# Target rows as three bfloat16 parts, one wait per gather pair, and one word of block numbers per chunk, in a graph attention and expert kernel

## The reference

```python
xl = (x @ W_l).reshape(n, H, C)          # n = 6250, H = 4, C = 64
xr = (x @ W_r).reshape(n, H, C)
feat = xl[src] + xr[dst]                 # 106250 edges, sorted by dst
feat = jnp.where(feat >= 0, feat, NEG_SLOPE * feat)
logits = jnp.einsum('ehc,hc->eh', feat, att)
seg_max = jax.ops.segment_max(logits, dst, num_segments=n)
ex = jnp.exp(logits - seg_max[dst])
seg_sum = jax.ops.segment_sum(ex, dst, num_segments=n)
alpha = ex / (seg_sum[dst] + 1e-16)
out = jax.ops.segment_sum(alpha[:, :, None] * xl[src], dst, num_segments=n)
```

## Time and profile before

| | us |
|---|---|
| median of three runs | 2654.8 (2643.6 to 2661.4) |
| the profiled execution, whole | 2630.2 |
| its span, first to last instruction | 2628.4 |
| mean granted TensorE clock | 0.903 |

### The profile page before, as it was taken

How to read it: one execution, slowest core, us unless ns; L and a number is a source line. 1 busy time by engine, 2 the same in 40 slices (tenths; PEclk the granted TensorE clock), 3 DMA queues, 4 the chain that set the end, 5 groups by cost and what they waited for, 6 DMA issues and landing times. The chain is left out here.

```text
span 2628.4 us, 46465 instructions
## 1 busy us (share of the span) xinstructions
PE 2168.0 (82%) x9585; PEld 1785.7 (68%) x9586; DVE 1553.9 (59%) x3448; ACT 1211.0 (46%) x3043; POOL 1351.4 (51%) x1265
## 2 busy tenths in 40 slices
PE   3967898988898899989998889853957719999993
PEld 2755777777677777777777767732846718888883
DVE  5745777777777777777777777887455420111110
ACT  2433556556565666656565655543541102222220
POOL 3356565666566666656665665446003762444442
PEclk9988999999999999999999999975965559999997
DMA  7555555555555555555555555434043345666664
GB/s 216 179 179 148 137 148 137 151 144 146 139 149 148 141 142 152 147 143 137 149 143 142 140 148 138 105 109 145 21 133 110 88 120 153 144 144 144 143 143 123
DMA packets 280941, 365.73 MB, mean 139 GB/s; under 512 B 52329, under 2 KB 233218, under 8 KB 280762
## 3 DMA queue, kind: packets, MB, share of 16 engines
q1 hardware_dynamic: 191070, 194.14, 25.5%
q0 software_dynamic: 73984, 154.20, 25.2%
q10 hardware_dynamic: 15836, 16.81, 2.0%
HBM read 306.42 MB, written 64.88 MB: 141 GB/s over the span
## 5 line engine op out<-in xcount | busy, mean ns | idle before, releaser
L773 POOL DMA_INDIRECT ring<-xl_rows,a_idx x928 | 927.2, 999 | 598.2 <-issue 239.0
L1078 PE MATMUL a_f_ps<-a_xr_w,a_hot_n 128*128 128x268 f32 x1856 | 595.4, 403 | 37.2 <-issue 13.1
L1091 PE MATMUL a_o_ps<-ring,a_hot_e 128*128 128x264 f32 x1856 | 508.7, 398 | 95.9 <-DVE acc L976 83.8
L1080 PE MATMUL a_f_ps<-ring,ident 128*128 128x264 f32 x1856 | 581.1, 396 | 0.0
L946 DVE SCALAR_TENSOR_TENSOR a_pos<-a_f_ps,att_ext 128x528 f32<-128x528 f32 x464 | 325.0, 700 | 374.2 <-PE a_f_ps L1080 238.4
L1091 PEld LDWEIGHTS a_o_ps<-ring,a_hot_e 128*128 128x128 f32 x1856 | 343.3, 193 | 185.4 <-issue 119.5
L1078 PEld LDWEIGHTS a_f_ps<-a_xr_w,a_hot_n 128*128 128x128 f32 x1856 | 355.9, 196 | 104.4 <-issue 42.9
L1080 PEld LDWEIGHTS a_f_ps<-ring,ident 128*128 128x128 f32 x1856 | 363.9, 196 | 72.6
L854 ACT COPY a_lg<-a_f_ps 128x8 f32<-128x8 f32 x464 | 79.2, 171 | 549.8 <-DVE a_pos L946 421.5
L956 DVE TENSOR_REDUCE a_lg<-a_pos 128x8 f32<-128x528 f32 x464 | 322.2, 694 | 1.4 <-issue 0.4
L964 DVE TENSOR_TENSOR ring<-ring (+1 forms) x464 | 316.8, 683 | 0.0
(11 more groups left out here) (306 smaller groups left out, 2198.1 us busy)
## 6 DMA issues: line engine op xcount, KB each, us to landing
a_xr_w<-xr_rows SPq DMA_DIRECT2D x464, 134.0 KB
a_rel_bc<-rel_rows SPq DMA_DIRECT2D x232, 128.0 KB
x_w<-in_L_ffn_W_dram SPq DMA_DIRECT2D x56, 512.0 KB
ring<-xl_rows,a_idx POOLq DMA_INDIRECT x928
ring<-disp_rows SPq DMA_DIRECT2D x56, 257.0 KB
xr_rows<-xr_sb SPq DMA_DIRECT2D x50, 134.0 KB, 1.9
xl_rows<-xl_sb SPq DMA_DIRECT2D x50, 132.0 KB, 1.8
j_xl<-xl_rows SPq DMA_DIRECT2D x25, 264.0 KB, 2.8
```

What stands on the lines that cost most here:

```text
L773: nc.gpsimd.indirect_dma_start(xl_e[:, p * T + 2 * h + u, :], None, k.xl_rows, bass.IndirectOffsetOnAxis(ap=idx[:, p, 2 * h + u:2 * h + u ...
L1078: nc.tensor.matmul(f_ps[:, g, u, 0:XRW], hot_n[:, j % 2, 2 * g + u, :], xr_w[:, h % XR, :], start=True, stop=False)
L1080: last = nc.tensor.matmul(f_ps[:, g, u, 0:XW], k.ident[:, :], xl_e[:, p * T + 2 * h + u, :], start=False, stop=True)
L1091: last = nc.tensor.matmul(o_ps[:, hh % 2, 0:XW], hot_e[:, j % 2, 2 * g + u, :], xl_e[:, pp * T + 2 * hh + u, :], start=(u == 0), stop=(u = ...
```

## The change

It has four parts.

1. `project_nodes` splits the 268 columns of each `xr` row in three bfloat16 parts: high = bf16(xr) on ACT (L627 in the new file), mid = bf16(xr - high) on DVE (L584), rest = xr - high on POOL (L541), low = bf16(rest - mid) on POOL (L546). `xr_rows` in DRAM then has 3 x 268 bfloat16 columns, and the store waits for the low part. The rings of `xl_sb` and `xr_sb` grow from four to eight.
2. `attend` multiplies a `hot_n` that is now bfloat16 with the three parts, adding up in PSUM; the identity product and the sums stay f32. The old L1078 is L1141, the old L1080 is L1143.
3. `gather` on POOL waits for `sum_done` alone, and for `idx_ready` in the first unit of a chunk.
4. `prepare_edges` packs the 16 block numbers of a chunk into a word (a block number and 15 bits), stores `word_rows`, and SP in `attend` reads one word per chunk and gets the numbers by register arithmetic. Some semaphores of `prepare_edges` are joined.

```diff
 def prepare_edges
@@ sync
                 sp.dma_start(k.block_rows[0].rearrange("(g u) -> g u", g=SG), blk_t[:, :]).then_inc(stored, 16)
+                sp.wait_ge(words_then_gates, 1)
+                sp.dma_start(k.word_rows[0].rearrange("(g c) -> g c", g=SG), word_i[:, :]).then_inc(stored, 16)
                 sp.wait_ge(ends_stored, 64)
@@ vector
+                link(nc.vector.memset(rise_bit[:, 1:2], float(WORD_BASE)))
+                for n in (1, 2, 4, 8):
+                    at = min(n, NU - 1 - n)
+                    link(nc.vector.tensor_scalar(rise_bit[:, 1 + n:1 + n + at], rise_bit[:, 1:1 + at], float(2 ** n), None, ALU.mult))
...
                 scales(nc, k, dve, link, 0, LN_HALF)
+                link(nc.vector.tensor_copy(blk_f[:, :, :], blk_t[:, :].rearrange("g (c h) -> g c h", h=NU)))
+                link(nc.vector.tensor_tensor(rise[:, :, 1:NU], blk_f[:, :, 1:NU], blk_f[:, :, 0:NU - 1], ALU.subtract))
+                link(nc.vector.tensor_tensor(rise[:, :, 1:NU], rise[:, :, 1:NU],
+                                             rise_bit[:, None, 1:NU].to_broadcast([SG, P // 2 // NU, NU - 1]), ALU.mult))
+                link(nc.vector.tensor_copy(rise[:, :, 0], blk_f[:, :, 0]))
+                link(nc.vector.tensor_reduce(blk_f[:, :, 0], rise[:, :, :], AX.X, ALU.add))
+                nc.vector.tensor_copy(word_i[:, :], blk_f[:, :, 0]).then_inc(words_then_gates, 1)
                 dve.wait_ge(picked[1], 16 * SG)
 def project_nodes
@@ sync
-                    sp.wait_ge(xr_full, t + 1)
+                    sp.wait_ge(low_ready, t + 1)
...
-                    sp.dma_start(k.xr_rows[bass.ds(row, P), :], xr_sb[:, s, :]).then_inc(stored[s], 16)
+                    sp.dma_start(k.xr_rows[bass.ds(row, P), :], parts[:, s].rearrange("p a w -> p (a w)")).then_inc(stored[s], 16)
@@ gpsimd
+                def rest_of(t, s):
+                    pool.wait_ge(high_ready, t + 1)
+                    wait_past(pool, low_ready, t - 1)
+                    nc.gpsimd.tensor_tensor(rest[:, s % 2, :], xr_sb[:, s, :], parts[:, s, 0, :], ALU.subtract).then_inc(rest_ready, 1)
+
+                def low_part(t, s):
+                    pool.wait_ge(mid_ready, t + 1)
+                    pool.wait_ge(rest_ready, t + 1)
+                    nc.gpsimd.tensor_tensor(parts[:, s, 2, :], rest[:, s % 2, :], parts[:, s, 1, :], ALU.subtract).then_inc(low_ready, 1)
@@ vector, at the end of self_logits(t)
+                    if not isinstance(t, int) or t >= 1:
+                        mid_part(t - 1, (s - 1) % ROWS)
+
+                def mid_part(t, s):
+                    dve.wait_ge(high_ready, t + 1)
+                    nc.vector.tensor_tensor(parts[:, s, 1, :], xr_sb[:, s, :], parts[:, s, 0, :], ALU.subtract).then_inc(mid_ready, 1)
@@ scalar, at the end of take_x(t)
+                    if not isinstance(t, int) or t >= 1:
+                        high_part(t - 1, (s - 1) % ROWS)
+
+                def high_part(t, s):
+                    act.wait_ge(xr_full, t + 1)
+                    nc.scalar.copy(parts[:, s, 0, :], xr_sb[:, s, :]).then_inc(high_ready, 1)
 def attend
@@ gpsimd, gather
-                    wait_past(pool, sum_done, c * NU + (h - RING + 1))
-                    wait_past(pool, f_done, c * NU + (h - LANDS + 1))
-                    pool.wait_ge(idx_ready, c + 1)
+
+                    if isinstance(c, int) and c * NU + h < RING:
+                        wait_past(pool, f_done, c * NU + (h - LANDS + 1))
+                    else:
+                        pool.wait_ge(sum_done, c * NU + (h - RING + 1))
+                    if h == 0:
+                        pool.wait_ge(idx_ready, c + 1)
@@ sync, loads
+                    word = nc.values_load_multi_w_load_instructions(k.row_words[:, bass.ds(c, 1)], engines=[mybir.EngineType.SP],
+                                                                    min_val=0, max_val=WORD_HALF - 1)[1][0]
+                    blocks = blocks_of(word)
                     for j in range(QUADS):
+                        row_of = [nc.sync.compute_val(blocks[2 * j + g]) for g in range(2)]
...
-                        blocks = load_blocks(nc, k, mybir.EngineType.SP, c * NU + 2 * j, 2)
@@ tensor, logits_of
                     for u in range(2):
-                        nc.tensor.matmul(f_ps[:, g, u, 0:XRW], hot_n[:, j % 2, 2 * g + u, :], xr_w[:, h % XR, :],
-                                         start=True, stop=False)
+                        for a in range(PARTS):
+                            nc.tensor.matmul(f_ps[:, g, u, 0:XRW], hot_n[:, j % 2, 2 * g + u, :], xr_w[:, h % XR, a, :],
+                                             start=(a == 0), stop=False)
```

More of the change, by code:

```diff
@@ L469, in project_nodes @@
         zt_sb = sb("zt_sb", [P, 2, 2, P])
-        xl_sb = sb("xl_sb", [P, RING, XW])
-        xr_sb = sb("xr_sb", [P, RING, XRW])
+        xl_sb = sb("xl_sb", [P, ROWS, XW])
+        xr_sb = sb("xr_sb", [P, ROWS, XRW])
+        parts = sb("xr_parts", [P, ROWS, PARTS, XRW], BF16)
+        rest = sb("xr_rest", [P, 2, XRW])
         f_sb = sb("f_sb", [P, 2, XW])
@@ L495, in _ @@
                         sp.dma_start(out[h * T:(h + 1) * T], rows[:, 0:NCH, :]).then_inc(k.fixed, 16)
-                tiles(sp, NTP, RING, RING, store)
-                sp.wait_ge(k.fixed, 16 * (1 + 2 * H))
-                for s in range(RING):
-                    sp.wait_ge(stored[s], 32 * len(range(s, NTP, RING)))
+                tiles(sp, NTP, ROWS, ROWS, store)
+                sp.wait_ge(k.fixed, 16 * (2 + 2 * H))
+                for s in range(ROWS):
+                    sp.wait_ge(stored[s], 32 * len(range(s, NTP, ROWS)))
             @block.gpsimd
@@ L603, in _ @@
                 project(NTP - 1, (NTP - 1) % 2)
-def load_blocks(nc, k, engine, at, n):
-    return nc.values_load_multi_w_load_instructions(k.blocks[:, bass.ds(at, n)], engines=[engine], min_val=0, max_val=NT - 1)[1]
-ADD = 27
-WORD_BASE = 64
-WORD_HALF = WORD_BASE * 2 ** (NU - 1)
 def pack_blocks(nc, k, link, rows, bits, bit):
```

87 lines of the change are left out of this document (56 added, 31 removed).

## The result

The changed kernel took 2667.03 us in the median of 17 runs (2655.52 to 2674.14); the kernel before, beside it on the same chip, 2655.60 us in the median of 17 (2643.64 to 2668.24). The ratio is 1.0038, 95% interval 1.0023 to 1.0054: slower by 0.4%, within what I had called no change. I had forecast 2631 us, faster than before. The range of 2570 to 2700 us held the result.

A forecast was written before the change was run, and what follows sets the result against it. PE was taken as the longest engine in the loop, though not by far, with PE and DVE pulling each other. Loop -67, projection +40, last tile +2, preparation +1 sum to -24 from 2654.8: about 2631 us, range 2570 to 2700.

The forecast's parts named there:

- PE's saving, 0.11 us a product, 102 us: Attention loop: three bfloat16 products take 0.34 us where the f32 product took 0.45, over 928 tiles.
- rival 3: Loop: a bfloat16 product costs 0.15 us because of its weight load, so the loop gains nothing; 2698 us, chance 0.08.
- -0.8 us per chunk: Loop, steps 0 to 5: DVE is late after its softmax work, PE waits more and loses 0.8 us of its saving.
- A late signal puts DVE back 2 us ... 0.4 us more per chunk: Loop: DVE starts after PE's needed product is long over, then gains 0.30 us per step on PE instead of 0.52.
- rival 5: Loop: DVE's chain sets the pace and PE only waits longer; 2698 us, chance 0.05.
- Bytes, 0 us: Loop: xr loads grow from 134 to 201 KB, 33 MB more in all, covered by eight buffers.
- One wait, one word, 0 us: Loop: the dropped gather wait was always met, and SP has time for its register work; no gain or loss.
- rival 4: Loop: late signals go with SP's traffic, half of 99 us gained on top; 2581 us, chance 0.12.
- POOL's 2.52 us a step: Loop: POOL's two gathers would pass PE's 2.46 us; PE's 1.4 us wait per chunk before the softmax covers the 1 us.
- Projection +40: Projection, 50 tiles: POOL's subtractions plus what DVE holds make a tile 3.0 us instead of 2.2; ends +10 and +70.
- Rival 2: Projection loses more than the loop gains; PE's clock may fall to 1.2 GHz, about 4 us a tile; 2708 us, chance 0.15.
- Rival 1: All of PE's 102 us saving arrives and POOL's start-up hides what DVE holds; 2566 us, chance 0.15.

The follow-up runs named there:

- e5: Changed kernel with xr rows loaded only for the first eight steps and rel rows twice, leaving SP little to issue: ratio 0.9937, loop 1523 us.
- e8: Changed kernel with two bfloat16 parts, the low part left out of the product: ratio 0.9935, loop 1545 us.
- e12: Kernel before with only one wait per gather pair in place of three: ratio 1.0001, loop 1340 us, no late starts.
- e13: Changed kernel unaltered, run again beside the kernel before: 2358.69 against 2409.36 us, ratio 0.9796, loop 1263 us.
- e15: Changed kernel with two bfloat16 parts, the low one left out, run again beside e13: ratio 0.9703, loop 1265 us.
- e3: Kernel before with only the single gather wait and the word of block numbers per chunk, xr kept float32: ratio 0.9952, loop 1544 us.
- e4: Changed kernel with xr rows loaded for the first eight steps only, 456 loads left out: ratio 1.0018, loop 1540 us.
- e1: Changed kernel issuing only the first of the three bfloat16 products in the loop: 2611.93 against 2627.30 us for before, ratio 0.9934.
- e7: Changed kernel with a fourth, unused bfloat16 product per tile into a spare bank: ratio 1.0093, loop 1558 us.

## Why the prediction was right or wrong

The step that failed is the price that I gave the late signals: 12 us, where they took 62 to 78 us, most or all of the loop's gain. On a chip without them the loop's terms came out right and the whole was faster, as forecast, but by 51 us and not by 24: the projection's term was 15 us too large, and the 12 us for late signals fell away. Step by step:

- **PE's saving, 0.11 us a product, 102 us.** Right: three records 0.114 us apart, 0.35 us until the next line, PE's step 2.47 us. The f32 weight load hides behind the third product; rival 3 is out. The Trainium skill's formula for the gap of an isolated matmul, in "TensorE: Matmul & The Clock Gate", section "Back-to-back issue gap", gives an estimate of 0.114 us for 268 columns, and this trace agrees with it in a stream of matmuls.
- **"-0.8 us per chunk" for VectorE's softmax.** Right: without late signals the steps h 1 to 5 take 3.88, 2.15, 3.52, 2.17 and 3.27 us in both kernels, VectorE's pace, and the chunk goes from 45.26 to 42.45 us: 2.8 of 3.5 us arrive.
- **"A late signal puts DVE back 2 us ... 0.4 us more per chunk".** This step failed. I took the late signals for a cost that stays the same and only delays the catching up: 12 us. They cost the kernel before 221 us of its loop (1561 against 1340) and the changed one 299 (1563 against 1263). The 78 us between are the whole saving; by the timed medians, 247 and 308 us, they are 62. That is 2.1 to 2.7 us a chunk in place of my 0.4. The time of late starts itself grows by less, from 260 to 293 us. What changes more is how much of it arrives, and that goes with the work that PE has to do. Medians of the group with e5 to e8 against those of the same kernels in the last group: the kernel before (PE step 2.68 us) loses 224 us, the one with the extra product (2.70) 214, though it has the most late starts, the one with two parts (2.24) 277. With the longer PE step VectorE has some 0.5 us in hand in each step in which it can catch up behind PE; with the shorter one (2.47) 0.3, with two parts hardly any. This reading fits the three losses, but no run varies the late signals by themselves.
- **Behind it, a reading.** I had written that of PE's missing 249 us in the loop "softmax products, some us of half clock" and waits for DVE were the causes, and given 99 us of remote waits as what the late signals hold. The loop holds 270 us of late starts, 9 us a chunk where I had 3.4. Most of the rest was booked under VectorE's wait for PE: of the 205.8 us in the earlier trace rows, 149 lie after the unit's own last L1080 was over. What VectorE really waited for PE's products, over the whole loop, is 91 us in the kernel before and 143 in e12, less with late signals than without. The argument against rival 5 ("DVE waits 205.8 us for PE") rested on that row and was worth little.
- **Bytes, 0 us.** Held as far as is shown: leaving all xr loads out gained 5 us by the ratios, 22 by the profiles. (The page has 35.8 MB more in all, not 33.)
- **One wait, one word, 0 us.** Held without late signals, 1.0000 and 1.0001. With them 12 us, so rival 4 had a grain of truth; but e5 shows that SP's traffic isn't their source.
- **POOL's 2.52 us a step.** Covered, as I had it: PE waits 11 us for gathers in e13. e15 is where it comes due.
- **Projection +40.** Right in its cause, too large: 22 us. A tile takes 2.62 and not 3.0 us. The term that was mis-sized is "what DVE holds is to be added": POOL's instructions grew from 0.775 to 0.84 us in the mean, 0.06 each and not 0.2. VectorE pays instead: g_sb 0.84 us and not the 0.9 that I had expected of z_sb (0.71) and the subtraction (0.59). The exclusion that the Trainium skill states in "SBUF — State Buffer", section "Who interferes with whom", shows in these rows on VectorE's side, where there was room.
- **Last tile +2.** It was 5: from the start of the last f_sb to the loop's first product 16.9 us, before 11.8. **Preparation +1:** it was about 0, the first f_sb starts at 57.7 us in place of 57.5.
- **Rival 2, the clock in the projection.** It did not come: the granted clock was 0.98 between 60 and 187 us. **Rival 1** did not come either: the loop gave at most 76 of the 102 us. **Rival 5** has the loop's length on the first chip right, but not the cause: with the same chain on DVE the loop of e13 is 76 us shorter.

With the measured terms: -76 for the loop, +22 and +5 for projection and last tile make -49; e13 stands 51 us under before. On the first chip the same edit has +27 in front of the loop and at most 16 us to set against it, of which e3's parts can be 12. That the result lies in the stated range is luck as far as the loop goes: an error of 51 to 67 us there (the saving that stayed away) stands beside one of 16 us the other way in front of it.

What stays open: what makes the signals late. It is in the loop only, on some chips; it stops VectorE, POOL and SP at the same moment and lets PE go on; it is not SP's issue (e5), not the xr loads (e4), not the number of code fetches (31 + 20 packets with late signals in e4, 94 + 20 without in e13). The gathers, which run in this stage throughout, were taken away in no run. Whether it is the chip itself or something that ran beside the kernel on it is not shown either: each group had one chip, and each was of one kind throughout. The loops' lengths come from single profiles, and e13 to e15 ran on one chip.

## What to carry to other kernels

Before pricing a shorter instruction, compare mean and median of each step of a loop: where the means lie far above (here 52.7 against 46.1 us over the 16 steps of a chunk), something outside the program's dependences may hold it, and work taken off the engine in front may be lost whole. Waits named after an engine are not evidence that this engine sets the pace, while others called remote stand beside them: measure from the end of the very instruction that the waiting one needs (here 149 of 205.8 us lay behind it). And set the fixed cost apart from the gain: the 27 us in front of the loop came on both kinds of chip, the gain in the loop on one.

## What the runs showed of the hardware

- The same kernel took 2409 us (spread 3 to 6 us) on two chips and 2627, 2633 and 2656 us (spread 24 to 27 us) in the other comparisons. All of it lies in one loop; what follows the loop took 889.5 to 892.0 us in every profile.
- In the slower ones SP takes 0.7 us for register arithmetic that takes 0.04 us in e13. In the place shown such a stretch ends at 765.5 us, and VectorE and POOL's sequencer go on within 0.2 us of it; at the earlier trace rows it ends at 1034.8 us, with VectorE's start. Emptying SP of transfers takes its slow records away (16 in place of 387) and leaves the late signals (130 in place of 127).
- There the granted clock of the loop was 0.91 to 0.97, lower the less PE had to do (1190 us of matmuls in e1 at 0.91, 1249 in e8 at 0.93, 1332 in the changed kernel at 0.95, 1395 in e7 at 0.97); without late signals it was 0.99 or 1.00 in every run, with PE busy 1240 us of 1264 as with 1323 of 1340.
- POOL's three instructions of 264 and 268 columns took 0.79 to 0.89 us beside VectorE's, where the one before took 0.775; it was VectorE's g_sb, with two inputs, that doubled, from 0.43 to 0.84 us.
